# Expert stage of a two-layer kernel: 96 of 128 tokens' one-hots by products, and TensorE's products in halves

## What is computed

```python
q = q.reshape(b, n, 2, H, KD).transpose(2, 0, 1, 3, 4)          # H = 8 heads, KD = 128
sim = jnp.einsum('pbnhd,hkpd->pbnhk', q, keys)                  # 2 x 32 keys
sx, ix = jax.lax.top_k(sim[0], 8); sy, iy = jax.lax.top_k(sim[1], 8)
all_scores = (sx[..., :, None] + sy[..., None, :]).reshape(b, n, H, 64)
all_indices = (ix[..., :, None] * 32 + iy[..., None, :]).reshape(b, n, H, 64)
scores, pk = jax.lax.top_k(all_scores, 8)
indices = jnp.take_along_axis(all_indices, pk, axis=-1)         # 8 of 1024 experts, per token and head
h = gelu_new(jnp.einsum('bnd,bnhkd->bnhk', x, down_embed[indices]))
h = jax.nn.softmax(scores, axis=-1) * h
out = jnp.einsum('bnhk,bnhkd->bnd', h, up_embed[indices])
```

## Time and profile before

| | |
|---|---|
| median of the three timed runs | 3096.15 us |
| profiled execution | 3113.54 us, of which the span is 3111.7 us |
| mean granted TensorE clock over the span | 0.899 |
| busy over the span | TensorE 91%, VectorE 75%, ScalarE 70%, GpSimd 58% |
| expert stage | about 1,940 to 2,893 us |

### The profile page before, as it was taken

One profiled execution on the slowest core, in us unless ns is written; L12 is line 12 of the kernel. 1 busy time (PEld: TensorE's weight loads), 2 busy tenths in 40 slices (PEclk: granted clock), 3 DMA queues, 4 the chain that ended last, 5 costly groups with the idle time before them and its releaser, 6 DMA issues. The chain is left out here.

```text
span 3111.7 us, 77365 instructions
## 1 busy us (share of the span) xinstructions
PE 2824.5 (91%) x27940; PEld 2094.8 (67%) x27940; DVE 2329.6 (75%) x8375; ACT 2190.7 (70%) x4267; POOL 1797.7 (58%) x1724
## 2 busy tenths in 40 slices
PE   5999999999999999999999995688898898988688
PEld 3777777777777777777777774466666666666443
DVE  5676766776766767767767645899999999998465
ACT  3887788788888887887787770465665566566575
POOL 3777777777778778778778780233333333332121
PEclk7999999999999999999999996677777787777799
DMA  3000000000000000000000002100000000000000
GB/s 101 1 1 8 1 1 8 1 1 8 1 1 8 1 1 8 1 1 8 1 1 8 1 1 86 42 0 0 0 0 0 0 0 0 0 0 1 1 28 28
DMA packets 11793, 27.63 MB, mean 9 GB/s; under 512 B 1529, under 2 KB 6137, under 8 KB 11137
## 3 DMA queue, kind: packets, MB, share of 16 engines
q1 hardware_dynamic: 11618, 25.48, 2.3%
HBM read 17.07 MB, written 8.40 MB: 8 GB/s over the span
## 5 line engine op out<-in xcount | busy, mean ns | idle before, releaser
L278 POOL TENSOR_TENSOR probs_l<-probs,probs_h 128x512 fp32r<-128x512 f32 x1024 | 1304.0, 1292 | 392.0 <-ACT probs_h L372 390.9
L371 ACT ACTIVATE probs<-bank 128x512 f32<-128x512 f32 x1024 | 625.0, 610 | 326.0 <-PE bank L692 299.7
L533 DVE TENSOR_REDUCE maxes<-ring 128x1 f32<-128x512 f32 x1024 | 659.0, 686 | 177.8 <-PE ring L672 176.9
L372 ACT ACTIVATE probs_h<-bank 128x512 fp32r<-128x512 f32 x1024 | 623.6, 609 | 0.0
L691 PE MATMUL bank<-q_hh,k_hl 128*128 128x512 f32 x1024 | 425.6, 416 | 0.2 <-ACT q_lm L361 0.2
L692 PE MATMUL bank<-q_lm,k_h 65*128 65x512 f32 x1024 | 406.9, 397 | 0.0
L702 PE MATMUL obank<-probs_h,x_l 128*128 128x512 f32 x1024 | 405.1, 396 | 0.0
L704 PE MATMUL obank<-probs_h,x_h 128*128 128x512 f32 x1024 | 404.6, 395 | 0.0
L703 PE MATMUL obank<-probs_l,x_h 128*128 128x512 f32 x1024 | 404.0, 395 | 0.0
L672 PE MATMUL ring<-k_hl,q_hh 128*128 128x512 f32 x1024 | 378.9, 431 | 25.0 <-DVE k_hl L517 6.6
L1063 ACT ACTIVATE low_hot<-obank 128x512 f16<-128x512 f32 x512 | 296.6, 603 | 71.7 <-PE obank L1229 58.9
(11 more groups left out here) (249 smaller groups left out, 4987.4 us busy)
## 6 DMA issues: line engine op xcount, KB each, us to landing
xt<-in_x SPq DMA_DIRECT2D x8, 512.0 KB, 9.7
out_x<-xt SPq DMA_DIRECT2D x8, 512.0 KB, 2.6
x<-out_x SPq DMA_DIRECT2D x1, 4096.0 KB, 12.1
out_x<-x SPq DMA_DIRECT2D x16, 256.0 KB, 2.1
mod<-out_x SPq DMA_DIRECT2D x3, 512.0 KB, 13.8
pk_wq<-in_w_q SPq DMA_DIRECT2D x1, 1024.0 KB, 4.9
pk_wqT<-in_w_qT SPq DMA_DIRECT2D x1, 1024.0 KB, 7.0
hot_rule<-in_hot_rule SPq DMA_DIRECT2D x1, 776.0 KB
```

The lines of the kernel that those rows point to most:

```text
L278: nc.gpsimd.tensor_tensor(probs_l[:, i, :], probs[:, s % 4, :], probs_h[:, i, :].bitcast(F32), ALU.subtract).then_inc(low_ready, 1)
L371: nc.scalar.activation(probs[:, s % 4, :], st[s % 4], ACT.Exp)
L372: nc.scalar.activation(probs_h[:, i, :], st[s % 4], ACT.Exp).then_inc(st_free[s % 4], 1)
L533: nc.vector.tensor_reduce(maxes[:, i, k:k + 1], ring[bank_of(at)][:], AX.X, ALU.max).then_inc(rows_maxed, 1)
```

## The change

OWN falls from 64 to 32: VectorE makes `low_hot` for 32 tokens of a pair, and 96 come by products (PARTS 3, BLOCKS 24). `expert_weights` is cut in two halves of 64 tokens. On TensorE the order of a pass is now: tokens 64 to 127 of pair u; turn_h, similarities, turn, activations of pair u+1 as before; the out products of tile 0 of pair u with the squares 6 to 14 of pair u+1, one behind each product; tokens 0 to 63 of pair u+1; the out products of tile 1 with the squares 15 to 23. No square stands in `expert_weights` any more. On ScalarE all squares of a pair are evicted in `middle`, and `back` comes behind the last. VectorE's `weigh` also waits for `out_full`, since z of the first 64 tokens would otherwise be written while tile 1's out products read it.

```diff
-OWN = 64
+OWN = 32
-BETWEEN = ((0, 3), (0, 7), (1, 1), (1, 3), (1, 5), (1, 7))
-GELU_AT, SUMS_AT, NEXT_AT = (4, 6), 12, 12
+GELU_AT = (4, 6)
...
@@ scalar
-                lows(u, GELU_AT[1], SUMS_AT)
+                lows(u, GELU_AT[1], BLOCKS)
...
                 middle(u + 1, True)
                 back(u)
-                lows(u + 1, SUMS_AT, BLOCKS)
...
@@ vector
             def weigh(u):
                 dve.wait_ge(g_ready, 2 * u + 2)
+                if not (isinstance(u, int) and u == 0):
+                    dve.wait_ge(out_full, u)
...
@@ tensor
-            def expert_weights(u):
-                pe.wait_ge(hots_ready, 2 * u + 2)
-                pe.wait_ge(g_ready, 2 * u + 2)
-                for t in range(P):
-                    if t % 8 == 0 and NEXT_AT + t // 8 < BLOCKS:
-                        low_square(u, NEXT_AT + t // 8)
+            def expert_weights(u, part):
+                if part == 0:
+                    pe.wait_ge(hots_ready, 2 * u + 2)
+                    pe.wait_ge(g_ready, 2 * u + 2)
+                for t in range(64 * part, 64 * part + 64):
                     if t >= OWN and t % 16 == 0:
                         pe.wait_ge(lows_read, BLOCKS * u + (t - OWN + 16) // 4)
...
+            def lows_after(u, q, e):
+                low_square(u, GELU_AT[1] + 9 * q + e + 1)
+
+            def combine(u, q):
+                if q == 0:
+                    pe.wait_ge(z_ready, 4 * u + 4)
+                    pe.wait_ge(gated_ready, u + 1)
...
+                nc.tensor.matmul(turn_bank[:, q * D:(q + 1) * D], ident[:], x2[:, 2 * u + q, :], start=True, stop=False)
+                if more:
+                    lows_after(u + 1, q, -1)
+                for e in range(8):
+                    mm = nc.tensor.matmul(turn_bank[:, q * D:(q + 1) * D], z[:, e, q, :], up_gated[:, e, :], start=False, stop=(e == 7))
+                    if q == 1 and e == 7:
+                        mm.then_inc(out_full, 1)
+                    if more:
+                        lows_after(u + 1, q, e)
...
             with pe.Fori(0, PAIRS - 2) as u:
-                expert_weights(u)
+                expert_weights(u, 1)
                 pe.wait_ge(stage_ready, u + 1)
                 turn_h(u + 2)
                 similarities(u + 2, 0)
                 turn(u + 1)
                 similarities(u + 2, 1)
                 activations(u + 1)
-                combine(u)
+                combine(u, 0)
+                expert_weights(u + 1, 0)
+                combine(u, 1)
```

More of the change, by code:

```diff
@@ L1086, in _ @@
             middle(0, True)
-            lows(0, SUMS_AT, BLOCKS)
             with act.Fori(0, PAIRS - 2) as u:
@@ L1104, in _ @@
             back(PAIRS - 2)
-            lows(PAIRS - 1, SUMS_AT, BLOCKS)
             back(PAIRS - 1)
@@ L1260, in expert_weights @@
                     if t >= OWN and t % 16 == 0:
                         pe.wait_ge(lows_read, BLOCKS * u + (t - OWN + 16) // 4)
-                    for part in range(2):
+                    for piece in range(2):
                         for q in range(2):
                             rows = slice(64 * q, 64 * q + 64)
-                            mm = nc.tensor.matmul(wide[q][:, 8 * t:8 * t + 8], low_hot[rows, t, :], value_hot[rows, t, part, :],
-                                                  start=(part == 0), stop=(part == 1))
-                            if t % 64 == 63 and part == 1:
+                            mm = nc.tensor.matmul(wide[q][:, 8 * t:8 * t + 8], low_hot[rows, t, :], value_hot[rows, t, piece, :],
+                                                  start=(piece == 0), stop=(piece == 1))
+                            if t % 64 == 63 and piece == 1:
@@ L1268, in expert_weights @@
                                 mm.then_inc(w_full, 1)
[L1270 to L1277, removed]
-                more = not (isinstance(u, int) and u == PAIRS - 1)
[L1279 to L1286, removed]
+            def lows_after(u, q, e):
+                low_square(u, GELU_AT[1] + 9 * q + e + 1)
@@ new lines, in combine @@
+            def combine(u, q):
+                if q == 0:
+                    pe.wait_ge(z_ready, 4 * u + 4)
+                    pe.wait_ge(gated_ready, u + 1)
+                    if isinstance(u, int) and u == PAIRS - 1:
+                        pe.wait_ge(out_read, u + 1)
+                    else:
+                        pe.wait_ge(coarse_ready, u + 2)
+                        pe.wait_ge(fine_ready, u + 2)
+                more = not (isinstance(u, int) and u == PAIRS - 1)
+                nc.tensor.matmul(turn_bank[:, q * D:(q + 1) * D], ident[:], x2[:, 2 * u + q, :], start=True, stop=False)
[7 more added lines that the diff above has]
+                        lows_after(u + 1, q, e)
@@ L1293, in _ @@
             activations(0)
-            for j in range(GELU_AT[1], NEXT_AT):
-                low_square(0, j)
+            for e in range(-1, 8):
+                lows_after(0, 0, e)
+            expert_weights(0, 0)
+            for e in range(-1, 8):
+                lows_after(0, 1, e)
             pe.wait_ge(x_back, 16 + 16 * len(later_loads))
             with pe.Fori(0, PAIRS - 2) as u:
-                expert_weights(u)
+                expert_weights(u, 1)
                 pe.wait_ge(stage_ready, u + 1)
@@ L1304, in _ @@
                 activations(u + 1)
-                combine(u)
-            expert_weights(PAIRS - 2)
+                combine(u, 0)
+                expert_weights(u + 1, 0)
+                combine(u, 1)
+            expert_weights(PAIRS - 2, 1)
             turn(PAIRS - 1)
             activations(PAIRS - 1)
-            combine(PAIRS - 2)
-            expert_weights(PAIRS - 1)
-            combine(PAIRS - 1)
+            combine(PAIRS - 2, 0)
+            expert_weights(PAIRS - 1, 0)
+            combine(PAIRS - 2, 1)
+            expert_weights(PAIRS - 1, 1)
+            combine(PAIRS - 1, 0)
+            combine(PAIRS - 1, 1)
         @block.gpsimd
```

## The result

The changed kernel takes 3303.78 us, the median of four runs (3303.55 to 3307.88), against 3096.36 us before: a ratio of 1.0667 (95% interval 1.0651 to 1.0683). The prediction was 3301.

The account below looks back on a forecast made before the run. VectorE, 97% busy, was taken as the bound before; afterwards ScalarE's late `float_ids` sets 34.9 us periods against 28.68. 28 periods add 174, plus 8, 10, 6 and 8: 206, scaled 205, giving 3301 us; eight in ten 3225 to 3360.

Parts of the forecast that it names:

- The place: ScalarE's queue: the next pair's `float_ids` and `exponentials` stand behind all squares and `back`, so GpSimd's slots reach VectorE late.
- The walk: One pair followed from its ids' transposition to the next: 34.02 us against 28.26, mean period 34.9; this case 65%.
- the clock's term: TensorE's clock may halve behind the first 64 tokens' products, slowing squares 15 to 23: bounds nothing to 2.4, taken 0.45.
- transposition to square 6 on ScalarE: Start of the walk: first square at 4.52, eviction +0.42, square 6 on ScalarE +7.00, thus 11.94 us.
- from `float_ids` to VectorE's product: ScalarE to GpSimd to VectorE: 2.36 us to the slots' end, 0.2 for VectorE to take them at L1140.
- from there to the next transposition: Walk's end: 4.63 us from L1140 to the split ids, about 0.1 to ScalarE, 0.47 to the transposition.
- The pace of squares at full clock: Low squares through two alternating banks on TensorE and ScalarE: two cost 1.18 us, one 0.59.
- VectorE runs one chain without a wait: Loop of the kernel before: VectorE is busy 679.8 of 700 us, returning to the same line one period later.
- rival 1: VectorE stays the bound and the change gains its 2.2 us, about 3030; needs `float_ids` within 16.4 us; 6%.
- It is not late again behind it: Behind L1140, gelu products fill the 2.5 us before VectorE's next one-hots; second-half one-hot products end 28.8, wanted 33.5.
- Outside the loop: Code around the loop, with cold one-hot products: +8 us ahead, first period 10, last about 6, +8 at the end.
- The scaling: Profiled execution 3113.5 us, timed median 3096.15, 0.56% less; so the added 206 us become 205.

Follow-up runs that it names:

- e9: e4 with ten products of a zero tile added in TensorE's two waits for ScalarE; 3242.9 us, ratio 1.0452.
- e6: Kernel before, with VectorE making the low one-hots of only 32 of its 64 tokens, the others left zero, still 16 squares; 3089.0 us, ratio 0.9956.
- e3: Changed kernel with the next pair's `float_ids` and `exponentials` moved on ScalarE to between squares 14 and 15; 3279.1 us, ratio 1.0569.
- e12: e11 with ten products of a zero tile added in TensorE's two waits for ScalarE; 3169.4 us, ratio 1.0209.
- e4: Changed kernel with the one-hot products uncut, all 128 tokens behind the squares and both tiles' out products; 3281.7 us, ratio 1.0578.
- e11: Changed kernel with OWN = 64 and 16 squares, `float_ids` and `exponentials` moved ahead of square 15; 3232.0 us, ratio 1.0412.

## Why the prediction was right, and where not

- **The place.** ScalarE's queue, with `float_ids` behind 24 squares and `back`: right. VectorE's wait ahead of the slots' product was forecast at 8 us a pair and is 8.7; ScalarE's idle time at the first half of the one-hot products was forecast at 3 and is 3.3.
- **The walk.** Forecast 34.9 a period with the clock's term, 35.07 measured. Term by term (means of 28 periods): transposition to square 6 on ScalarE 11.94 forecast, 11.88 measured; the 64 tokens' products 3.46, 3.40; from `float_ids` to VectorE's product 2.56, 2.39; from there to the next transposition 5.20 forecast, 5.63 measured, of which 0.43 is the pairs with the gate product, which I had carried over as 0.42. Each of these held within 0.2.
- **Two terms were mis-sized, and each hid part of the other.** The pace of squares at full clock: I built 1.18 for two from reaction times, 1.08 was measured, 0.7 less over both groups. The cost of the clock: I put 0.45 a pair, it is 1.7 (0.6 in the squares 7 to 14, 0.9 in 16 to 23, 0.2 at square 15). Together they leave the walk 0.5 too short, and the other terms, most of them a little shorter than forecast, give some 0.4 of it back: that the total came within 0.2 of 35.07 is in part luck. I had looked for the fall behind the first half of the one-hot products only and missed the other place, where TensorE waits for ScalarE's gelus. It could have been seen beforehand: square 6 goes into the bank of square 4, which ScalarE reads only behind the first gelu. In the kernel before, x and four out products stand ahead of it and the wait is 0.67; now only the product with x does, and it is 1.56. The rule of the Trainium skill that I cited ("TensorE: Matmul & The Clock Gate", The HAM clock gate), that activity alone lifts the throttled state, points the same way as e9: with products of zeros in these waits the clock stays full among the squares.
- **What bounds the kernel before.** "VectorE runs one chain without a wait" is true, but I took from it that VectorE is the bound. e6, whose period falls by 0.5 us only, shows that TensorE's chain takes nearly the same 28.3 us. It stands in the rows I had chosen: 23.5 from the transposition to the end of the one-hot products (2487.23 to 2510.76) and 4.7 to the next. It made no difference to the forecast, since the change lengthens both; but rival 1, worth 66 us as I priced it, could have brought some 20 at most (the 14 of e6 and 6 for its waits for the slots). Its margin was also added up wrongly: by the walk `float_ids` starts 25.0 us behind the start of the low one-hots (26.26 less 1.25), not 24.3, which makes that case no likelier. e3 shows that moving `float_ids` forward recovers one per cent, not six. "It is not late again behind it" was nearly false: ScalarE has only 0.30 us between the similarities and the split ids.
- **Outside the loop.** Forecast +18 ahead of the loop and in its first pass, 6 and 8 at the end: measured 14.7, 5.4 and 6.5. The gaps where one-hot products run for the first time were there (0.9 to 1.9 us).
- **The scaling.** I scaled the profiled execution's sum to the median by 0.56%. The profiled execution after took 3303.55, its median: what the one before had on top lay ahead of the expert stage (17.1 us) and was no property of the stage. The 206 us of the stage, without any scaling, are the difference of the medians, 207.

## What to carry to other kernels

When an engine is busy to 97%, take its work away in an experiment before trading for it: here 2.1 us of 28.3 were worth 0.5, since a chain through the other engines took just as long. Walk the one full period from an event back to itself through each queue, with what stands ahead of each instruction; it gave most terms of this change's price to within 0.2 us; the squares' pace and the clock were off by more. And where a reordering leaves TensorE to wait in a stretch of dense products, price that stretch at both clocks.

## What the runs showed of the hardware

- Adding work made the kernel faster: ten products of zeros a pair (2.2 us of TensorE) in its waits saved 1.2% in e9 and 2.0% in e12, by keeping the granted clock at full there. Without them the clock fell to half in a part of the pairs at 1.56 and 1.23 us of waiting with 1.1 us between; in the other pairs it stayed full over the same waits.
- Which pairs fall follows a pattern, for the most part: 32.7, 38.5, 35.1, 33.7 in turn in the changed kernel, 32.6 and 35.6 in turn in e4, 34.1 again and again in e11. The fall makes a pair longer, and that may move the place of the next one; no run here shows what decides it.
- The small one-hot products hardly feel the clock: 256 take 3.37 us at full and 3.58 at the most, with the granted clock at 0.50 over them. From the start of a square to the next product it is 0.22 us at full and 0.43 at half.
